# Post-norm ViT block with a mixture of experts: units of 256 rows, four to a chunk, and rows put side by side by ScalarE

## The reference

```python
h = patches @ W.T + b + pos                      # (32, 1024, 64)
q, k, v = h @ Wq.T + bq, h @ Wk.T + bk, h @ Wv.T + bv
a = softmax(where(mask, q @ k.T / 8, -1e9)) @ v @ Wo.T + bo
x = layernorm(h + a)
probs = softmax(x @ gate_w + gate_b); idx = argmax(probs)      # 8 experts
pos = place of the token among those of its expert, in order   # kept if pos < C = 5120
y = (relu(x @ w1[idx] + b1[idx]) @ w2[idx] + b2[idx]) * prob * kept
out = layernorm(x + nan_to_num(y))
```

## Time and profile before

| | us |
|---|---|
| median of 3 runs (lowest, highest) | 1235.28 (1235.03, 1239.02) |
| the profiled execution's own time | 1234.83 |
| its span | 1233.0 |
| PE busy in the span | 1041.4 (84%) |
| DVE, POOL, ACT busy | 919.1, 718.3, 650.8 |

### The profile page before, as it was taken

The page is one execution under the profiler, slowest core; times in us unless marked ns, Lnnn a source line. Parts: engine busy times, 40 slices in busy tenths (PEclk is TensorE's granted clock), DMA queues, the critical chain, the costliest instruction groups (busy, mean ns, idle before and its releaser), DMA issues.

```text
span 1233.0 us, 17442 instructions
## 1 busy us (share of the span) xinstructions
PE 1041.4 (84%) x5036; PEld 534.8 (43%) x5036; DVE 919.1 (75%) x1927; ACT 650.8 (53%) x880; POOL 718.3 (58%) x712
## 2 busy tenths in 40 slices
PE   3899999999999999999999999999989873345530
PEld 2455555555455555555554555554544431111210
DVE  4667778778989898988888988888888664535541
ACT  2355554555666666666666666666656541223320
POOL 0014555444676767666766676767675776536655
PEclk9999999999999999999999999999999976677775
DMA  5334433444444444444444443434351202222300
GB/s 122 88 77 124 105 91 76 111 112 100 106 109 107 106 102 107 105 106 104 105 106 109 99 117 94 123 93 124 76 126 35 70 16 75 74 61 72 89 12 2
DMA packets 102661, 112.02 MB, mean 91 GB/s; under 512 B 54350, under 2 KB 78919, under 8 KB 102566
## 3 DMA queue, kind: packets, MB, share of 16 engines
q1 hardware_dynamic: 85158, 93.78, 31.5%
q0 software_dynamic: 17408, 17.12, 4.6%
HBM read 42.20 MB, written 19.30 MB: 50 GB/s over the span
## 4 chain that ended last, share of the span: by engine, by line
PE 55%; DVE 25%; issue 9%; another core or an unknown queue 5%; ACT 2%; DMA 1%; POOL 1%; SPq 1%; POOLq 0%; DVEq 0%; ACTq 0%
PE p_u L562 15%; PE p_st L546 8%; DVE mx L929 8%; PE p_st L549 7%; PE p_sm L532 5%; PE p_misc L518 4%; PE p_misc L497 4%; PE p_misc L577 3%; PE p_misc L623 3%; PE p_misc L638 2%; DVE ld L980 1%; DVE b_o L1135 1%; DVE b_p L1084 1%; DVE b_n L1100 1%
## 5 line engine op out<-in xcount | busy, mean ns | idle before, releaser
L1263 POOL DMA_INDIRECT slots<-rows,idx x256 | 265.0, 1035 | 236.1 <-issue 147.2
L1275 POOL DMA_INDIRECT out<-b_o,b_ix x288 | 304.3, 1056 | 138.7 <-issue 77.6
L929 DVE TENSOR_REDUCE mx<-p_sm 128x1 f32<-128x1024 f32 x252 | 307.3, 1219 | 89.8 <-PE p_sm L532 82.5
L751 ACT ACTIVATE pT<-p_st 128x1024 f32<-128x1024 f32 x256 | 262.1, 1024 | 186.7 <-PE p_st L549 98.9
L562 PE MATMUL p_u<-pT,vv 128*64 128x512 f32 x1024 | 263.5, 614 | 0.0
L546 PE MATMUL p_st<-mQ,sK 128*128 128x512 f32 x512 | 183.6, 440 | 5.3 <-ACT pT L751 3.4
L549 PE MATMUL p_st<-mR,sR 72*128 72x512 f32 x512 | 161.1, 395 | 0.0
L532 PE MATMUL p_sm<-sK,mQ 64*128 64x512 f32 x252 | 139.9, 555 | 12.8 <-DVE mx L929 8.2
L532 PE MATMUL p_sm<-hi,mQ 64*128 64x512 f32 x252 | 139.8, 555 | 0.0
L546 PEld LDWEIGHTS p_st<-mQ,sK 128*128 128x128 f32 x512 | 79.4, 189 | 104.2 <-issue 79.4
L623 PE MATMUL p_misc<-b_xT,b_w 64*128 64x512 f32 x244 | 79.3, 730 | 34.1 <-issue 19.2
(11 more groups left out here) (181 smaller groups left out, 1492.8 us busy)
## 6 DMA issues: line engine op xcount, KB each, us to landing
mQ<-hi SPq DMA_DIRECT2D x64, 256.0 KB
b_in<-slots SPq DMA_DIRECT2D x72, 132.0 KB
b_x<-slots SPq DMA_DIRECT2D x72, 128.0 KB
sK<-hi SPq DMA_DIRECT2D x32, 256.0 KB
sK<-lo SPq DMA_DIRECT2D x32, 256.0 KB
mR<-lo SPq DMA_DIRECT2D x32, 256.0 KB
sR<-hi SPq DMA_DIRECT2D x32, 256.0 KB
xt<-in_x SPq DMA_DIRECT2D x32, 196.0 KB
```

Of the source, the lines that this page charges most:

```text
L751: act.activation(pT[k % 4][:, :], flat(p_st), ACT.Exp).then_inc(exp_done, 1)
L929: dve.tensor_reduce(mx[:, p, j:j + 1], flat(max_place(n, j)), AX.X, ALU.max).then_inc(max_done, 1)
L1263: pool.indirect_dma_start(slots, bass.IndirectOffsetOnAxis(ap=idx[:, p, j:j + 1], axis=0), rows[:, p, j, :], None, bounds_check=SLOTS - 1, ...
L1275: pool.indirect_dma_start(out_rows, bass.IndirectOffsetOnAxis(ap=b_ix[:, o, j:j + 1], axis=0), b_o[:, o, j, :], None, bounds_check=T - 1, ...
```

## The change

A unit has 256 rows, and a chunk is two *pairs* of units: still 1024 rows, so `b_in`, `b_x`, `b_xT`, `b_h` and `b_yT` hold as much of a chunk as before. There are 128 full units plus at most 8 partial ones: NC = 34 chunks. `HOST` starts at 6, so 27 chunks lie inside steps 6 to 32 and 7 in rounds; `LAST` is 29, so two rounds come before the two empty ones and five behind them.

Per unit SP now issues three DMAs (the rows once, into `b_in`; w1; w2), 12 per chunk, and reads four table entries. A new ACT activation, `rows_beside`, copies the 64 features of all rows of the chunk from `b_in` to the single buffer `b_x`, in which the two units of a pair lie side by side. In a step it stands behind `qk_high` and ahead of the first exponential; in a round ahead of `xT_copy`. `rows_turn` waits for it. `up` and `down` issue twice as many matmuls of 256 columns, `rectify` four activations of 256 per f and not two of 512, `sums_copy` two and not one.

```diff
-UNIT = 512
+UNIT = 256
 UT = UNIT // P
-CHR = 2 * UNIT
+PAIRS = 2
+CT = PAIRS * UT
-NC = (NB * S // UNIT + E) // 2
-HOST = [*range(8, NB + 1)]
+NC = (NB * S // UNIT + E) // 4
+HOST = [*range(6, NB + 1)]
...
-        if c < n - 3:
+        if c < n - 1:
...
-        b_x = sb("b_x", [P, NBUF, UT, 2 * D])
+        b_x = sb("b_x", [P, CT, 2 * D])
...
-                for u in range(2):
-                    sp.dma_start(b_x[:, r, :, u * D:(u + 1) * D], unit_rows(at[u])[:, :, 0:D])\
-                        .then_inc(c_loaded[r], 16)
-                    sp.dma_start(b_in[:, r, u, :, :], unit_rows(at[u])).then_inc(c_loaded[r], 16)
...
+                for k in range(2 * PAIRS):
+                    v, u = k // 2, k % 2
+                    t = slice(v * UT, (v + 1) * UT)
+                    sp.dma_start(b_in[:, r, u, t, :], unit_rows(at[k])).then_inc(c_loaded[r], 16)
+                    sp.dma_start(b_w1[u * D:(u + 1) * D, r, v, :],
...
-                pe.wait_ge(c_loaded[r], 128 * (c // NBUF) + 128)
+                pe.wait_ge(c_loaded[r], 96 * PAIRS * (c // NBUF + 1))
+                pe.wait_ge(b_x_ready, c + 1)
...
-                for u in range(2):
-                    h = slice(u * D, (u + 1) * D)
-                    pe.matmul(place[:, u, :], b_w1[h, r, f * P:(f + 1) * P], b_xT[h, :], start=True, stop=True)\
-                        .then_inc(b_h_done, 1)
+                for v in range(PAIRS):
+                    for u in range(2):
+                        h = slice(u * D, (u + 1) * D)
+                        pe.matmul(place[:, u, v * UNIT:(v + 1) * UNIT], b_w1[h, r, v, f * P:(f + 1) * P],
+                                  b_xT[h, v, :], start=True, stop=True).then_inc(b_h_done, 1)
...
+            def rows_beside(c):
+
+                r = c % NBUF
+                act.wait_ge(c_loaded[r], 96 * PAIRS * (c // NBUF + 1))
+                if c >= 1:
+                    act.wait_ge(b_t_done, c)
+                act.activation(b_x[:, :, :].rearrange("p j (u d) -> p u j d", d=D), b_in[:, r, :, :, 0:D], ACT.Copy)\
+                    .then_inc(b_x_ready, 1)
...
                 for u in range(2):
-                    act.wait_ge(b_h_done, 2 * HB * c + 2 * f + u + 1)
-                    act.activation(b_h[:, f, u, :], place[:, u, :], ACT.Relu,
-                                   bias=b_w2[:, r, u, HB * D + f:HB * D + f + 1]).then_inc(b_relu, 1)
+                    act.wait_ge(b_h_done, 2 * PAIRS * (HB * c + f) + 2 * (PAIRS - 1) + u + 1)
+                    for v in range(PAIRS):
+                        act.activation(b_h[:, f, u, v, :], place[:, u, v * UNIT:(v + 1) * UNIT], ACT.Relu,
+                                       bias=b_w2[:, r, v, u, HB * D + f:HB * D + f + 1]).then_inc(b_relu, 1)
...
                 if has(2):
                     qk_high(b + 2, par, c % 3, third(0))
+                if m is not None:
+                    rows_beside(m)
...
                     if c is not None:
+                        rows_beside(c)
                         xT_copy(c)
```

More of the change, by code:

```diff
@@ L71 @@
 TABLES = sorted(set(IMAGE))
-TAKEN = [2 * IMAGE.count(n) for n in TABLES]
+TAKEN = [4 * IMAGE.count(n) for n in TABLES]
 STARTS = [sum(TAKEN[:i]) for i in range(len(TABLES))]
@@ L312, in build @@
         c_loaded = [sem(f"c_loaded{i}") for i in range(NBUF)]
+        b_x_ready = sem("b_x_ready")
         b_t_done = sem("b_t_done")
@@ L406, in load_chunk @@
                 at, e = [], []
-                for u in range(2):
-                    named = sp.value_load(tab[0:1, 2 * c + u:2 * c + u + 1], min_val=0,
+                for u in range(2 * PAIRS):
+                    named = sp.value_load(tab[0:1, 2 * PAIRS * c + u:2 * PAIRS * c + u + 1], min_val=0,
                                           max_val=PACK * (E - 1) + DUMMY)
@@ L465, in _ @@
             for r in range(NOUT):
-                sp.wait_ge(b_scattered[r], 16 * NT * NC // NOUT)
+                sp.wait_ge(b_scattered[r], 16 * NT * len(range(r, NC, NOUT)))
         @block.tensor
@@ L590, in rows_turn @@
                     pe.wait_ge(b_xT_ready, c)
-                for j in range(UT):
-                    last = pe.transpose(banks(c)[0][:, j * P:(j + 1) * P], b_x[:, r, j, :], c_id[:, :])
+                for j in range(CT):
+                    last = pe.transpose(banks(c)[0][:, j * P:(j + 1) * P], b_x[:, j, :], c_id[:, :])
                 last.then_inc(b_t_done, 1)
@@ L599, in turn_back @@
                     pe.wait_ge(b_p_ready, c)
-                for j in range(UT):
-                    last = pe.transpose(place[:, j * P:(j + 1) * P], b_yT[:, j * P:(j + 1) * P], c_id[:, :])
+                for j in range(CT):
+                    last = pe.transpose(place[:, j * P:(j + 1) * P], b_yT[:, j // UT, j % UT * P:(j % UT + 1) * P], c_id[:, :])
                 last.then_inc(b_back_done, 1)
@@ L635, in down @@
                     pe.wait_ge(b_yT_ready, c)
-                for f in range(HB):
-                    for u in range(2):
-                        last = pe.matmul(place[u * D:(u + 1) * D, :], b_w2[:, r, u, f * D:(f + 1) * D],
-                                         b_h[:, f, u, :], start=(f == 0), stop=(f == HB - 1))
+                for v in range(PAIRS):
+                    for f in range(HB):
+                        for u in range(2):
+                            last = pe.matmul(place[u * D:(u + 1) * D, v * UNIT:(v + 1) * UNIT],
+                                             b_w2[:, r, v, u, f * D:(f + 1) * D], b_h[:, f, u, v, :],
+                                             start=(f == 0), stop=(f == HB - 1))
                 last.then_inc(b_y_done, 1)
@@ L770, in xT_copy @@
                 if c >= 1:
-                    act.wait_ge(b_h_done, 2 * HB * c)
-                act.activation(b_xT[:, :], banks(c)[0], ACT.Copy).then_inc(b_xT_ready, 1)
+                    act.wait_ge(b_h_done, 2 * PAIRS * HB * c)
+                act.activation(b_xT[:, :, :].rearrange("p v r -> p (v r)"), banks(c)[0], ACT.Copy)\
+                    .then_inc(b_xT_ready, 1)
             def rectify(c, f):
@@ L787, in sums_copy @@
                     act.wait_ge(b_back_done, c)
-                act.activation(b_yT[:, :], banks(c)[2], ACT.Identity, bias=b_w1[:, r, FF:W1C])\
-                    .then_inc(b_yT_ready, 1)
+                act.activation(b_yT[:, 0, :], banks(c)[2][:, 0:UNIT], ACT.Identity, bias=b_w1[:, r, 0, FF:W1C])
+                act.activation(b_yT[:, 1, :], banks(c)[2][:, UNIT:2 * UNIT], ACT.Identity,
+                               bias=b_w1[:, r, 1, FF:W1C]).then_inc(b_yT_ready, 1)
             def squares(c):
```

31 lines of the change are left out of this document (15 added, 16 removed).

## The result

| | before | changed |
|---|---|---|
| median of 20 runs each, taken in turn | 1236.44 us | 1227.53 us |
| the profiled execution's own time, its span | 1234.83, 1233.0 | 1224.63, 1222.8 |

The ratio is 0.9911 [0.9888, 0.9933]: 11 us faster (1236.44 x 0.0089; the two medians differ by 8.9), where 30 were forecast. The time lies 1.5 us above the range. The direction was right and the size was not.

A forecast was written before the change was run, and what follows sets the result against it. PE was taken to bound the steps, a chain through ACT, DVE and PE plus stalls the rounds. Span 1233.0 + 11.1 + 8 + 5 - 54 = 1203.1, so 1205 us; range from 3 below 1190 to 1226.

The forecast's parts named there:

- Two more chunks inside: In the steps: two full steps of 31.5 us replace two of 25.9, adding 11.1 us.
- Smaller matmuls: In PE-bound steps: doubled matmul records cost 0.3 us a chunk, +8 us over 27 steps, with ends of 4 and 26.
- The saving is 0: Loads in the steps: half the small row pieces save 0, since DMA, 43% busy, is not the limit.
- no stall in the steps: Steps: no stall there, as POOL never issues more than a dozen without other work; no cost was put on it.
- Way in: From 1000 to 1077 us, into the rounds: four more DMA issues (+2.8) and copy with transposes (+1.7), +5 us.
- upper case: Upper end, 15 us, for the way into the rounds: the next load, issued inside the stall, takes 2.4 us a DMA, +10.
- A round: Undisturbed round: copy, transposes and smaller items add 2.0 to 2.7 us to the chain, 12.3 us and not 9.9.
- The rounds behind `LAST`: Tail: five chunks and not nine, 92.2 us plus 10 of stalls, 102.2 against 156.2, so -54 us.
- A: Rounds and the way in: stalls go altogether and the way in is not lengthened, 1190 us; chance 0.20.
- B: Rounds: SP's loads bound them, 11.8 us a chunk, and stalls come back to 35 us; 1230 us; chance 0.12.
- C: Matmuls, mainly in steps: weight loads are not hidden, costing 26 us and not 8; 1223 us; chance 0.12.
- D: Head of the steps: ACT's copy waits for late loads and stops the attention chain; slower, 1251 us; chance 0.06.

## Why the forecast was wrong, point by point

The profiled span is 1222.8 us and 1203.1 were forecast, 19.7 more. The steps give 10.4 of them (29.5 and not 19.1), the way in 5.4 (10.4 and not 5), the rounds behind `LAST` 3.9 (50.1 less and not 54). The 10.4 hide a larger miss: the 19.1 had 8 us for smaller matmuls that cost nothing, so stretched steps, which had been put at nothing, cost 18.9 (29.5 less the 10.6 between the two kernels without stalls).

**Two more chunks inside, +11.1: right.** 10.6 between the kernels in sets without stalls.

**Smaller matmuls, +8: wrong, it is 0.** Steps take the same with twice the records; the 16 of `down` take 1.95 us where 8 took 1.94. The Trainium skill's full load of weights ("TensorE: Matmul & The Clock Gate", "LDWEIGHTS (loading the stationary operand)"), unhidden, is out: at the prediction's 1.3 us a chunk every step would be longer by it. That most steps took the forecast 31.8 in the first profile is luck: there nearly every second step, 30.5 in the sets without stalls, is stretched to 31.5 or more.

**"The saving is 0" of the loads in the steps, and "no stall in the steps": this failed, and it is the step that matters most.** From step 6 to step 31 the changed kernel takes 802.5 and 799.0 us with stalls and 777.4 and 777.1 without: 22 to 25 more. The kernel before takes 772.8 to 776.1 with stalls (four traces) and 767.3 without: 6 to 9 more. Between the two kernels of the result the difference is 19 us, nearly all that was missing (13 in the other set that has a trace of each, there with the few scatters and the pauses of the tail). I priced SP's 12 issues as if a stall could only fall into rounds, and gave no reason why the steps should stay free of them. That the issues lie beside the long steps is seen; that they cause them wasn't shown, and the cause stays open.

**Way in, +5: mis-sized, +10.4.** Its upper case came in part: the next load's first DMAs are issued inside the stall, at 1073.37, 1077.64, 1081.87 and 1085.39. But the stall is the smaller part of it. Without stalls the way from step 31 to the same `up` takes 95.1 us in the changed kernel and 86.5 before, already 8.6 more, and the stalls add only the other 2. I priced one load and one copy, but all of its rounds grow: 21.6, 12.4 and 21.5 us lie between their `b_yT`, and 17.6, 8.5 and 17.9 before.

**A round, 12.3: wrong base, right addition.** The addition of 2.0 to 2.7 is 2.1 (10.6 against 8.5). But both kernels change clock in the rounds. The 9.9 of the earlier trace rows is an 8.5 us chain, partly at 1.2 GHz (`up` takes 1.99 and 1.91 in it, and 1.13 in a round of 8.5). In the changed kernel PE waits longer, and where `down` is at 1.2 GHz as well the round is 13.3 to 13.6; where it isn't, 11.6 to 12.4. That 12.3 lies between them is luck. In four later rounds it is only +1.8 in sum, because the first took 10.1. The four halved activations take 1.57 us, where 1.4 was taken; the Trainium skill's budget ("ScalarE: Activation LUTs", "Rules for kernel authors") makes 2.0, an estimate that the trace puts too high here.

**The rounds behind `LAST`, -54: -50.1.** 14 us of stall and not 10, at its head. I read the ACT chain as the bound with POOL equal to it. Where there are no stalls POOL is the bound of the kernel before, whose 14 chunks of scatters take 155 us, and chain and POOL share the tail of the changed one. The -52.9 that this part measures there is near my -54 by luck. That scatters come with stalls is shown (few scatters take them away). That breaks thin them is likely and not shown: the later rounds have none, and pauses in the kernel before left 37 us and not 92. The rows of 24 at the head of the tail stayed, and every stall behind 1000 us is beside one; a third such row, from 1183.55, has none beside it. Over the whole span the stalls cost the changed kernel more: before loses some 45 us in such a set (1236 against 1191), the changed one some 64 (1227.5 against 1164).

**The rivals.** A falls: 34.6 us of remote waits are left behind 1000 us. (Where there are no stalls the kernel before has none either, and the gain is 27 to 29 us.) B falls for 12 issues a chunk: fewer loads change nothing measurable in either kernel, and 14 us of stall came back and not 35; with 16 issues the rounds do wait for loads. C falls: smaller matmuls cost nothing. D falls: in the steps the copy never waits for a load, and stands right behind `qk_high`:

```profile
451.10 1.02 ACT L735 ACTIVATE hi<-p_misc 128x1024 fp32r<-128x1024 f32 x1 [2.92 <-PE p_misc L499]
452.02 0.62 ACT L780 ACTIVATE b_x<-b_in 128x512 f32<-128x512 f32 x1
```

It waits for one once, in the first round:

```profile
1060.13 0.63 ACT L780 ACTIVATE b_x<-b_in 128x512 f32<-128x512 f32 x1 [4.22 <-DMA b_w<-in_w]
```

**Open:** what the remote waits are in the hardware, why only some sets have them and whether it is the chip, and whether scatters, loads or both stretch the steps there. No run changed the scatters or the loads of the stretched steps in a set with stalls.

## What to carry to other kernels

When a tail drains through a queue, count what that engine still has to issue from the last full stage to the end (here 112 scatters at 1.39 us) beside the compute chain, in the kernel before and in the one after: the bound can change hands. Two chunks less in the tail brought 10 us while the round got longer, the next two 34, and a chain up to 3 us a round faster brought 7 us in all. A wait that a trace shows without a reason should enter a forecast as a cost that can move into the stage that grows, not only as one that shrinks. Measure a pair more than once, some time apart: the same two kernels have a ratio of 0.991 in one set and 0.977 in another.

## What was not expected of the hardware

- The same kernel takes 1236 or 1191 us, by the set. In the tail the difference comes with POOL's output scatters: with one of eight left, 5.0 us of remote waits remain of 92.3, and 1159.78 us.
- In the changed kernel's rounds of 13.6 us PE waits 3.1 and 2.3 us, and `down` behind them runs at 1.2 GHz, 3.58 us for 1.95; with eight idle matmuls of 256 columns in a round PE stayed at 2.4 GHz, and a round is 10.6 us.
- A POOL product of 1.06 us lies beside every DVE addition that takes 2.0 to 2.2 and not 0.69 us. The Trainium skill has the two share a port pair that the holder locks ("SBUF — State Buffer", "Who interferes with whom"); the trace agrees that one of them waits, by 1.46 us in the addition shown. In that run work was taken off POOL, its product moved, and the kernel was 19 us slower than with the same work taken off in the tail alone.
